# Four transformer layers on one core: raw rows for the first projection, ranks a step later, weights from another queue, values behind the cosines

## What is computed

```python
x = x + attention0(layernorm(x))   # 16 heads of width 8, q and k of unit length, softmax, no mask
x = x + experts0(layernorm(x))     # 8 experts, the best one per row, gelu, width 32
x = x + attention1(layernorm(x))   # 16 heads of width 64, causal softmax, output projection
x = x + experts1(layernorm(x))     # 8 experts, the best two per row, gelu, width 512
x = layernorm(x) * gamma + beta    # the last block's own end
```

## Time and profile before

| | us |
|---|---|
| median of three runs (1430.69 to 1435.87) | 1434.65 |
| the profiled execution's own time | 1436.96 |
| its span, first to last instruction | 1434.8 |
| TensorE busy | 1257.9 (88%) |
| VectorE busy | 872.1 (61%) |
| ScalarE busy | 837.9 (58%) |
| GpSimd busy | 596.5 (42%) |

### The profile page before, as it was taken

The page is one execution under the profiler, slowest core; times in us unless marked ns, Lnnn a source line. Parts: engine busy times, 40 slices in busy tenths (PEclk is TensorE's granted clock), DMA queues, the critical chain, the costliest instruction groups (busy, mean ns, idle before and its releaser), DMA issues.

```text
span 1434.8 us, 28298 instructions
## 1 busy us (share of the span) xinstructions
PE 1257.9 (88%) x9316; PEld 783.9 (55%) x9316; DVE 872.1 (61%) x3100; ACT 837.9 (58%) x1593; POOL 596.5 (42%) x775
## 2 busy tenths in 40 slices
PE   3878799999999999999999999999888887988791
PEld 1323355555555555555555556555555555978791
DVE  4464655667675766676667666665666562543384
ACT  3765676677656756675667566755533443544362
POOL 1000133343445344343534254335445455676585
PEclk8978999999999999999999999999989999999996
DMA  9042092000000000000000000000001021465662
GB/s 343 1 179 83 8 5 2 1 8 1 8 9 17 1 8 14 10 8 1 16 8 9 1 16 1 8 3 14 1 21 77 1 88 46 141 193 180 193 213 93
DMA packets 76589, 73.01 MB, mean 51 GB/s; under 512 B 42296, under 2 KB 52928, under 8 KB 76320
## 3 DMA queue, kind: packets, MB, share of 16 engines
q1 hardware_dynamic: 71904, 61.84, 18.1%
q0 software_dynamic: 4544, 9.38, 1.9%
HBM read 39.38 MB, written 31.81 MB: 50 GB/s over the span
## 4 chain that ended last, share of the span: by engine, by line
PE 56%; DVE 15%; ACT 9%; issue 9%; POOL 7%; POOLq 2%; DMA 0%; another core or an unknown queue 0%; SPq 0%; DVEq 0%
PE scores L1737 12%; PE outs L1755 9%; PE outs L1884 7%; PE work L1677 7%; PE work L1784 4%; DVE scores L1244 3%; PE scores L1871 3%; DVE ra L1237 3%; ACT a_buf L960 3%; PE scores L1706 3%; ACT ra L966 2%; POOL choice_rows L906 2%; POOL big L884 2%; PE work L1857 2%; PE work L1845 2%
## 5 line engine op out<-in xcount | busy, mean ns | idle before, releaser
L1244 DVE CUSTOM_DVE_ANT_0 scores<-scores,mask_qk 128x512 f32<-128x512 f32 (+3 forms) x512 | 238.9, 519 | 173.7 <-PE scores L1706 173.5
L954 ACT ACTIVATE big<-scores 128x1024 f32<-128x1024 f32 (+1 forms) x192 | 169.8, 885 | 231.1 <-PE scores L1737 226.8
L801 POOL TENSOR_SCALAR_AFFINE_SELECT big<-big 128x256 f32<-128x256 f32 x256 | 101.2, 408 | 468.4 <-ACT big L954 438.0
L960 ACT ACTIVATE a_buf<-scores 128x1024 f32<-128x1024 f32 x256 | 248.1, 1029 | 44.5 <-PE scores L1871 44.2
L1737 PE MATMUL scores<-ra 64*128 64x512 f32 (+3 forms) x1536 | 184.3, 345 | 13.0 <-ACT a_buf L960 4.7
L821 POOL TENSOR_TENSOR big<-big 128x768 f32<-128x768 f32 x64 | 116.6, 1822 | 133.9 <-issue 53.6
L1737 PEld LDWEIGHTS scores<-ra 64*128 64x128 f32 x1536 | 121.6, 187 | 63.6 <-issue 41.5
L1755 PE MATMUL outs<-big 128*64 128x512 f32 (+3 forms) x1024 | 154.1, 443 | 0.0
L1884 PE MATMUL outs<-a_buf 128*16 128x512 f32 x1024 | 146.8, 648 | 2.0 <-ACT a_buf L960 1.8
L1237 DVE TENSOR_TENSOR ra<-work,ra 128x512 fp32r<-128x512 f32 x128 | 88.4, 691 | 89.8 <-ACT ra L966 89.7
L1028 ACT ACTIVATE big<-scores,b_sb 128x128 f32<-128x128 f32 x312 | 88.0, 368 | 83.9 <-PE scores L1938 57.6
(11 more groups left out here) (222 smaller groups left out, 2343.1 us busy)
## 6 DMA issues: line engine op xcount, KB each, us to landing
a_buf<-in_w SPq DMA_DIRECT2D x78, 256.0 KB
sorted_rows<-xrows SPq DMA_DIRECT2D x34, 520.0 KB, 6.8
qkT<-sorted_rows SPq DMA_DIRECT2D x78, 65.0 KB
a_buf<-in_x SPq DMA_DIRECT2D x8, 256.0 KB, 2.7
x_rows<-x SPq DMA_DIRECT2D x8, 256.0 KB
a_buf<-in_w SPq DMA_DIRECT2D x1, 2048.0 KB, 8.0
ra<-x_rows SPq DMA_DIRECT2D x8, 256.0 KB
a_buf<-choice_rows SPq DMA_DIRECT2D x6, 256.0 KB, 3.7
```

What stands on the lines that cost most here:

```text
L954: activation(prob1(g, i), d[:, :, 0:256] if i == 2 else d, ACT.Exp, scale=SCALE1).then_inc(unit_free("pair", g, i), 1)
L960: activation(prob0(c)[:, i * 1024:(i + 1) * 1024], unit_wait(act, "cosine", c, i), ACT.Exp).then_inc(unit_free("cosine", c, i), 1)
L1244: return v.tensor_tensor_reduce(scores_, scores_, mask_qk[:, SEQ - width:SEQ], -1.0, 3e38, ALU.add, ALU.min, neg_max[:, qt, j:j + 1])
```

## The change

- The host also gives x transposed (`x_T0`). SP loads it to `xT_h`; `rows_h`, its standardization, transposes and copy go. Before all else TensorE sums the columns of the q, k and v weights with ones and VectorE subtracts their mean, so that the projection of raw rows is free of the row's mean; `qkv_moved` multiplies by the row's `rstd`.
- Ranks are counted in step 6 behind "sum" and moved after `normalize`; in step 5 `normalize` comes behind x_lo.
- `values0` of cosine(0) stands behind `max_transposed` and `cosines` of cosine(1) in every pass.
- First weights of the tiles are loaded from ScalarE's queue, six tiles ahead, the first six in step 6 of pass 7; SP loads rows alone. The table entry is read once, there.
- In the tile loops: x3 of the last batch is stored at SP's tile 22 and the reloads start at 13, one in three tiles; the last batch's rows are scattered one transfer per tile from 24 on; the finish starts four tiles later, every third tile, with three buffers of deviations instead of two. `x_T_moved(0)` goes to step 7 of pass 7, ahead of `normalize`.
- At the end the additions of x3 stand behind the deviations on GpSimd, and that of the last batch is VectorE's.

```diff
-W1_RING = RING
+W1_RING, W1_AHEAD = RING, 6
-AT_TABLES, AT_SEND, AT_KEPT, AT_BACK = 23, 25, 26, 30
+AT_TABLES, AT_SEND, AT_KEPT, AT_BACK = 23, 24, 22, 13
-FINISH_AT, FINISH_EVERY = LATE.tile + 5, 4
+FINISH_AT, FINISH_EVERY = LATE.tile + 9, 3
...
     add(o.pair(-1), ("sum", o.pair(-1)))
...
+    if p == 6:
+        add(t, ("rank", t))
     add(o.pair(2), ("k", o.pair(2)))
     add(o.pair(1), ("mT", o.pair(1)))
...
-        add(h, ("xT0", h))
...
-    if p == 5:
-        add(t, ("rank", t))
...
         @block.sync
+            def next_x_T(h):
+                if h:
+                    work_wait(sp, "qkv0", h - 1, TILES - 1)
+                sp.dma_start(xT_h, x_T0[h]).then_inc(x_T_loaded, 16)
...
+            next_x_T(1)
             def next_x(h):
                 sp.wait_ge(x_taken, h - 1)
                 sp.dma_start(x_in(h), x[h]).then_inc(x_loaded[h % 2], 16)
+                next_x_T(h)
...
-                if n >= W1_RING:
-                    sp.wait_ge(hidT_full, n - W1_RING + 1)
-                cols = sp.value_load(expert_at[0:1, n:n + 1], min_val=0,
-                                     max_val=(EXPERTS - 1) * HID1)
-                sp.dma_start(w1_tile(n), w1_1[:, bass.ds(cols, HID1)]).then_inc(
-                    w1_tile_in[n % W1_RING], 16)
...
                 if n == AT_BACK:
+                    sp.wait_ge(kept, 16 * LAST_T)
+                if n == AT_BACK + 3 * LAST_T:
                     sp.wait_ge(kept, 16 * BATCH)
-                if AT_BACK <= n < AT_BACK + BATCH:
-                    sp.dma_start(x3_kept(n - AT_BACK), x3_rows[n - AT_BACK]).then_inc(x3_back, 16)
+                b, k = divmod(n - AT_BACK, 3)
+                if k == 0 and 0 <= b < BATCH:
+                    sp.dma_start(x3_kept(b), x3_rows[b]).then_inc(x3_back, 16)
...
         @block.gpsimd
-                if AT_SEND <= n < AT_SEND + TILES:
-                    send_rows(LAST_T, (n - AT_SEND,))
+                if AT_SEND <= n < AT_SEND + TILES * CHOICES:
+                    send_rows(LAST_T, ((n - AT_SEND) // CHOICES,), ((n - AT_SEND) % CHOICES,))
...
             for b in range(LATE.first, LATE.last):
-                inverse_deviations("fin", b, b % 2)
-                if b > LATE.first:
-                    add_x3(b - 1)
-            add_x3(LAST_T)
+                inverse_deviations("fin", b, b % 3)
+            for b in range(LATE.first, LAST_T):
+                add_x3(b)
...
         @block.scalar
                 w = work_wait(act, "qkv0", h, t)
-                copy(qk0(h).rearrange("p (w t n) -> p w t n", w=2, t=TILES)[:, :, t, :],
-                     w[:, 0:2 * DIM].rearrange("p (w n) -> p w n", w=2))
+                act.wait_ge(rstd_ready["a0"], h + 1)
+                activation(qk0(h).rearrange("p (w t n) -> p w t n", w=2, t=TILES)[:, :, t, :],
+                           w[:, 0:2 * DIM].rearrange("p (w n) -> p w n", w=2), ACT.Copy,
+                           scale=rstd[:, 1, t:t + 1])
...
+            def weights_wanted(n):
+                chunks[n] = act.value_load(chunk_at[0:1, n:n + 1], min_val=0,
+                                           max_val=(EXPERTS - 1) * CH1)
+                if n >= W1_RING:
+                    act.wait_ge(hidT_full, n - W1_RING + 1)
+                act.dma_start(w1_tile(n), w1_1[:, bass.ds(chunks[n] * P, HID1)]).then_inc(
+                    w1_tile_in[n % W1_RING], 16)
...
-                if (o.i, p) == (LAST_PASS, 0):
+                if (o.i, p) == (LAST_PASS - 1, 6):
                     act.wait_ge(tables_ready, 1)
+                    for n in range(W1_AHEAD):
+                        weights_wanted(n)
                 if o.pair(-1) is not None:
                     inverse_sums(o.pair(-1))
...
                 hidden_gelu(n)
+                if n + W1_AHEAD < ALL_TILES:
+                    weights_wanted(n + W1_AHEAD)
...
         @block.vector
+            dve.wait_ge(sums_full, 1)
+            v.scalar_tensor_tensor(wqkv0_sb[:], outs[:, 0, 0:3 * DIM], -1.0 / DIM, wqkv0_sb[:],
+                                   ALU.mult, ALU.add).then_inc(weights_centred, 1)
...
+                if (o.i, p) == (LAST_PASS - 1, 7):
+                    x_T_moved(0)
                 if (o.i, p) == (LAST_PASS, 0):
-                    for n in range(3):
-                        x_T_moved(n)
+                    x_T_moved(1)
+                    x_T_moved(2)
                 if o.pair(-1) is not None and p != 5:
                     normalize(o.pair(-1))
...
-                if p == 3 and h is not None:
-                    standardize("a0", h, x_in(h), rows_h)
...
-                if p == 5 and t is not None:
+                if p == 5 and o.pair(-1) is not None:
+                    normalize(o.pair(-1))
+                if p == 6 and t is not None:
                     ranks_moved(t)
-                if p == 6 and t is not None:
                     slots1(t)
                     gates1(t)
...
-            scaled(LAST_T)
+            link(scaled(LAST_T))
+            v.tensor_tensor(chosen(LAST_T, 0), chosen(LAST_T, 0), x3_kept(LAST_T),
+                            ALU.add).then_inc(out_last, 1)
...
         @block.tensor
             pe.wait_ge(first_in, 16 * 2)
+            pe.wait_ge(consts, 1)
+            pe.wait_ge(out_free[1], 1)
+            for j in range(2):
+                last = mm(outs[j * D1:(j + 1) * D1, 0, 0:3 * DIM], ones[:], wqkv0_sb[:], start=True,
+                          stop=True)
+            last.then_inc(sums_full, 1)
...
+                if p == 6 and t is not None:
+                    ranks1(t)
 
                 if o.pair(2) is not None:
                     project("k", 1, o.pair(2))
-                if o.cosine(0) is not None and o.i >= 0:
-                    values0(o.cosine(0))
                 if o.pair(1) is not None:
                     max_transposed(o.pair(1))
                 if o.cosine(1) is not None:
                     cosines(o.cosine(1))
-                if o.cosine(0) is not None and o.i < 0:
+                if o.cosine(0) is not None:
                     values0(o.cosine(0))
...
-                if p == 4 and h is not None:
-                    pe.wait_ge(rows_ready["a0"], h + 1)
-                    transposes(rows_h, "xT0", h)
...
-                if p == 5 and t is not None:
-                    ranks1(t)
```

More of the change, by code:

```diff
@@ L259 @@
 X_IN = VSTAT + 2 * TILES * H0 * VCOLS
-ROWS_H = X_IN + 2 * SEQ
-XT_H = ROWS_H + SEQ
+XT_H = X_IN + 2 * SEQ
 NORMS = XT_H + SEQ
@@ L840, in second_rows, with send_rows @@
                 nc.gpsimd.tensor_copy(xrows[:, :, 1, 0:DIM], xn).then_inc(rows_full, 1)
-            def send_rows(t, tiles):
-                if 0 in tiles:
+            def send_rows(t, tiles, choices=range(CHOICES)):
+                if 0 in tiles and 0 in choices:
                     pool.wait_ge(rows_full, t + 1)
@@ L850, in send_rows @@
                 for tile in tiles:
-                    for k in range(CHOICES):
+                    for k in choices:
                         nc.gpsimd.indirect_dma_start(
@@ L1566, in _ @@
                     operand_moved(1, s, 3)
-                if p == 5 and o.pair(-1) is not None:
-                    normalize(o.pair(-1))
                 if p == 5 and f is not None:
```

63 lines of the change are left out of this document (35 added, 28 removed).

## The result

The changed kernel takes 1420.52 us (median of 13 runs, 1417.36 to 1431.67) where the kernel before takes 1435.02 (13 runs): a ratio of 0.9907, with a 95% interval of 0.9886 to 0.9929. That is 14.5 us less where 23.6 were forecast. The profiled execution took 1421.36 us (span 1419.6), 15.6 less than that of before.

The account below looks back on a forecast made before the run. TensorE was taken to bound the middle passes (work for 129.6 of 136 us), stalls to cost some 36 us in the tile stage. Terms summed to -23.6 us, from 1434.65 to 1411; own range 1403 to 1419, with A, B, C 1399 to 1428.

Parts of the forecast that it names:

- Startup: Before the first projection: standardization, transposes and a copy leave the path; -1.5 us, between -3 and +1.
- Transposes, values and ranks in the steps: Passes: transposes of x gone -3.0 us, maxima uncovered by moved values +2.9, ranks moved to step 6 +2.2.
- Weights to ScalarE's queue: Step 6 of pass 7: six load issues delay ScalarE's logarithm and TensorE, mostly covered by GpSimd's scatters; +0.8 of 0 to +5.
- Tile stage: Last quarter, 54 tiles: 139.1 us where 102.6 would do; four stretches together -23.0 us.
- First stretch: Sends 24 to 35: SP's queue of weights, rows and x3 reloads relieved, GpSimd's scatters stay; -8.7 us, bounds 0 and -14.2.
- Second: Sends 35 to 51: one SP issue a tile instead of two at 1.08 us each; -4.8 us.
- Third: Sends 51 to 56: VectorE's 9.5 us wait for chosen rows goes, first sum four tiles later and SP ahead; -9.5 us.
- Fourth: Sends 56 to 77: GpSimd sends rows and finishes batches, same work packed in fewer tiles; 0 us.
- Tail: End of kernel: GpSimd's addition no longer delays the last reciprocal deviation, last addition goes to VectorE; -2.0 us.
- A: Rival: the steps lose more, every maxima wait uncovered (+4.5 us) and ranks at their upper bound (+5.8); 1421 us, chance 0.13.
- B: Rival: bytes, not issues, hold the tile stage's first two stretches, which keep their times; 1425 us, chance 0.14.
- C: Rival: VectorE still waits for chosen rows, so sends 51 to 56 keep their time; 1420 to 1421 us, chance 0.08.

Follow-up runs that it names:

- the controls: The kernel before and the changed kernel, both unchanged, run beside follow-up experiments on another chip; the changed kernel took 1412.11 us, ratio 0.9939.
- the second group: Follow-up kernels run together on another chip, with the kernel before and the changed kernel both unchanged; the changed kernel took 1412.11 us, ratio 0.9939.

## Why the prediction was right, and where its sizes were off

The forecast was faster by over 0.5%, and it is; 1420.5 lies in the range of 1399 to 1428 but 1.5 us outside the forecast's own, 1403 to 1419. In the second group it is 0.6% faster (0.4 to 0.8), so the direction is sure and the 0.5% is not quite. Point by point, against the profiled pair:

- **Startup**, -1.5 forecast. The first projection starts 3.4 us earlier and pair 0 stands 1.8 earlier, 3.0 in the controls. With 152 to 159 us for that mark over all traces, the term is neither shown nor refuted.
- **Transposes, values and ranks in the steps**, +2.1 forecast, +3.5 measured up to pair 62 (from -1.8 to +1.7). The parts: the ranks' old wait was 2.1 a pass as said; the new one 2.2, not 2.8, released by VectorE's `ranks_moved` as said. The values' order costs 0.9 us a pass, not 0.41: besides three waits of 0.3 to 0.4 us for the maxima, the transposes wait 0.2 us in three more steps for a bank that ScalarE frees. With -0.6 for the transposes of x that gives +0.4 a pass; passes without a fallen clock went from 136.4 to 137.1 us in the second group, +0.7. The transposes' term was not tried alone, and the 0.3 us a pass between the two stay open. The fallen clock, which the forecast left out, doesn't show in this sum only because it stood behind the old wait as often as behind the new one.
- **Weights to ScalarE's queue**, +0.8 forecast. This is the first size that failed, and the clearest. The chain was named in full (six issues of 1.08 us, logarithm, bank, transposes, projection) and bounded at +5; the value taken rested on "GpSimd's scatters of routed rows already hold the next step". Moving the issues behind the copy gave 5 us: nothing held it. Of the cover that was claimed no row had been read that ends later than the delayed work.
- **Tile stage**, -23.0 forecast, -18.8 measured. First stretch -4.1 for -8.7, and here the cause fails too. The forecast read two row loads 5.2 us apart as three issues in one queue. In the second group the kernel before has the same three issues a tile, and its row loads come 2.7 us apart:

```profile
1275.93 0.33 SPq L690 DMA_DIRECT2D qkT<-sorted_rows  x1
...
1277.39 0.46 SPq L726 DMA_DIRECT2D ra<-x_rows  x1
1278.62 0.33 SPq L690 DMA_DIRECT2D qkT<-sorted_rows  x1
```

  There the stretch takes 28.5 us, and the change takes 0.6 off; with the weights on SP again it takes 1.6 more. So of the 14.2 us lost in the first profile 6.7 are pauses that come with the set of runs, about 7 are GpSimd's scatters ("5.5" in the forecast), and without pauses next to nothing is left for SP's queue. The 4.1 us gained in the first pair are mostly shorter pauses (6.7 us before, about 3 after). What slows SP's issues in them, and whether the change shortens them or the two traces differ by chance, isn't shown. Second -6.6 for -4.8: GpSimd catches up there at under 1.90 us a tile. Third -11.0 for -9.5. Fourth +2.9 for 0 (46.1 us to the start of send 77, then 49.0): "the work is the same, packed in fewer tiles" overlooked that GpSimd is full there, so that five finishes in fewer tiles only shift time from the third stretch to the fourth. GpSimd is busy 43.4 of the 49.0 us:

```profile
1347.80:1396.80 49.00, 39.65 (x327) 38.32 (x326) 34.22 (x126) 28.77 (x96) 43.38 (x50) 0.93 0.56 182
```

  The cause given for the third was half wrong as well. With SP relieved and the finish at its old place the stretch takes 12.3 us, so SP's relief brings some 7 of the 11; the four tiles of distance bring the rest, and the fourth stretch takes that back.
- **Tail**, -2.0 forecast, 25.1 to 22.8 us measured, and the same in the controls. The deviation of the last batch now starts at 1410.90 with no addition ahead of it, unlike the earlier trace rows:

```profile
1410.90 1.45 POOL L804 TENSOR_TENSOR rstd<-var_eps,minus_half 128x4 f32<-128x4 f32 x1 [1.13 <-DVE var_eps L1230]
```

- **Rivals.** A gave 1421, almost the time measured, but by another way: the steps cost 1.4 us more than forecast, not 10. That it came so near is luck. B falls as a mechanism: with the same bytes issued by SP the stretches get longer by 16.7 us in sum, and in the changed kernel the DMA share rose from 0.56 to 0.73 in the second stretch and to 0.90 in the third. Its outcome for the first stretch, that it keeps its time, did come true in the second group, but by GpSimd's scatters. By the rule of the Trainium skill (DMA: Bandwidth & Descriptors, "Issuing engines are not separate DMA queues") issuing from several engines saves only the issuing engine's time, which is usually small beside the transfer. Here that time was what counted: 1.1 us an issue, two issues for a tile of 1.90 us, 19.6 us in all. C: the wait for chosen rows is gone. D: no sign of it. Of the signs that the forecast named one failed: the first stretch runs at 2.8 us a tile, above 1.9 to 2.4.

## What to carry to other kernels

Before a delay is counted as covered, find the row of the covering work that ends later than the delayed one will; a cover named in general is a guess. Before a gap between two issues is put down to the queue, see whether other stretches or traces with the same issues have it. Before two moves in the same step are priced one by one, ask whether one takes away what would hide the other's wait. And where an engine is full, as GpSimd in the finish, moving the work in time only moves the loss; moving it to another engine removes it.

## What had not been expected of the hardware

- A TensorE wait of 2.1 to 2.2 us between full stretches was followed in 8 of 10 passes of the first two profiles by a granted clock of about 0.5 for 3.4 to 6.8 us, 1.5 to 1.6 us lost for one of 3.4; over all traces it was 39 of 50, and each fall began between 1.2 us before the end of the wait and 1.6 us behind it. Behind a wait of 1.2 us in the same place it never fell in five passes.
- Six back-to-back DMA issues hold ScalarE's instruction stream for 5.7 us; nothing behind them in its order starts meanwhile.
- The same two kernels differ by 1% between groups of runs, in part by pauses of three engines at once in tiles 28 to 35, in part by a wait of 0.6 to 0.7 us a pass for ScalarE's exponentials. The cause of both stays open.
